# Five PSUM banks shared out anew between two kinds of attention scores in one layer

## The reference

```python
x = x + layernorm(attention(layernorm(x)))        # layer 1: 16 heads of 8, rotary, causal
x = x + layernorm(block2(layernorm(x)))
# block2: y = x + attention(rmsnorm(x))           # layer 2: 16 heads, latent keys (16) and 32 rotary columns
#         y + shared expert + top 2 of 8 experts, on rmsnorm(y)
```

## Time and profile before

| | |
|---|---|
| median of 3 runs | 577.48 us (576.83 to 578.33) |
| the profiled execution | 578.05 us, span 576.0 us |
| busy: PE, DVE, ACT, POOL | 507.3, 412.2, 313.7, 200.6 us |
| PE matmul instructions | 3168 |
| exps (L853) | 320, 600 ns each |
| maxima with mask (L1231) | 256, 638 ns each |
| plain reduces (L1221) | 96, 692 ns each |
| fills' matmuls, layer 1 (L530) | 256, 303 ns each |
| units' matmuls, layer 1 (L559) | 237 recorded, 295 ns each |
| HBM traffic | 80 GB/s over the span |

### The profile page before, as it was taken

How to read it: one execution, slowest core, us unless ns; L and a number is a source line. 1 busy time by engine, 2 the same in 40 slices (tenths; PEclk the granted TensorE clock), 3 DMA queues, 4 the chain that set the end, 5 groups by cost and what they waited for, 6 DMA issues and landing times.

```text
span 576.0 us, 9488 instructions
## 1 busy us (share of the span) xinstructions
PE 507.3 (88%) x3168; PEld 276.7 (48%) x3190; DVE 412.2 (72%) x1209; ACT 313.7 (54%) x586; POOL 200.6 (35%) x268
## 2 busy tenths in 40 slices
PE   7888988978899888999999999998989798899784
PEld 3433443433443344556565556554756346553643
DVE  6689898798589976876686688766476764554465
ACT  2485685767656775656756646543355342654131
POOL 5432643365236541564336414421032000410010
PEclk9999999999999999999999999999999899999978
DMA  5455524114223432448345542532203200000001
GB/s 139 128 147 172 149 82 138 43 44 135 77 80 117 155 72 90 91 115 171 103 99 108 121 127 91 129 46 52 53 15 66 55 2 1 20 2 0 2 1 37
DMA packets 29672, 47.17 MB, mean 82 GB/s; under 512 B 4648, under 2 KB 15144, under 8 KB 29112
## 3 DMA queue, kind: packets, MB, share of 16 engines
q1 hardware_dynamic: 28496, 45.72, 31.0%
q10 hardware_dynamic: 1128, 0.85, 0.7%
HBM read 27.22 MB, written 18.87 MB: 80 GB/s over the span
## 4 chain that ended last, share of the span: by engine, by line
PE 54%; DVE 27%; ACT 10%; issue 5%; POOL 3%; DVEq 0%; ACTq 0%; POOLq 0%
PE ps L612 11%; PE ps L565 9%; DVE ps L1231 8%; PE ps L686 8%; PE ps L532 6%; PE ps L530 4%; PE ps L820 3%; DVE NM L1221 3%; DVE terms L1337 2%; PE ps L550 2%; ACT PG L853 2%; PE ps L559 2%; PE ps L737 2%; PE ps L667 1%; DVE stats L1205 1%
## 5 line engine op out<-in xcount | busy, mean ns | idle before, releaser
L853 ACT ACTIVATE PG<-ps 128x512 f32<-128x512 f32 x320 | 179.4, 600 | 139.0 <-PE ps L565 87.7
L1231 DVE CUSTOM_DVE_ANT_0 ps<-ps,below 128x512 f32<-128x512 f32 (+1 forms) x256 | 157.1, 638 | 45.2 <-PE ps L532 22.6
L565 PE MATMUL ps<-QS,K 128*128 128x512 f32 x320 | 115.4, 445 | 3.0 <-ACT PG L853 2.9
L612 PE MATMUL ps<-PG,V 128*32 128x512 f32 (+3 forms) x1024 | 95.0, 444 | 3.1 <-DVE ON L1278 1.8
L532 PE MATMUL ps<-K,QS 96*128 96x256 f32 (+3 forms) x256 | 74.1, 341 | 10.2 <-DVE NM L1231 9.9
L1221 DVE TENSOR_REDUCE NM<-ps 128x2 f32<-128x512 f32 (+1 forms) x96 | 65.5, 692 | 22.1 <-PE ps L550 18.3
L530 PE MATMUL ps<-KS,QS 96*128 96x256 bf16 (+3 forms) x256 | 64.5, 303 | 17.3 <-DVE NM L1231 13.2
L565 PEld LDWEIGHTS ps<-QS,K 128*128 128x128 f32 x320 | 53.9, 189 | 44.1 <-ACT PG L853 23.1
L1066 POOL TENSOR_TENSOR rstd<-ve,half 128x4 f32<-128x4 f32 x20 | 20.4, 1018 | 117.4 <-DVE ve L1213 83.2
L1174 POOL TENSOR_SCALAR_AFFINE_SELECT PG<-PG 128x512 f32<-128x512 f32 x64 | 39.6, 641 | 57.4 <-ACT PG L853 57.0
L1167 POOL TENSOR_SCALAR_AFFINE_SELECT PG<-PG 128x512 f32<-128x512 f32 x64 | 38.7, 638 | 49.5 <-ACT PG L853 49.5
(11 more groups left out here) (170 smaller groups left out, 679.4 us busy)
## 6 DMA issues: line engine op xcount, KB each, us to landing
scr<-QC SPq DMA_DIRECT2D x24, 512.0 KB, 2.8
QS<-scr SPq DMA_DIRECT2D x64, 128.0 KB
scr<-room SPq DMA_DIRECT2D x20, 256.0 KB, 2.6
QS<-scr SPq DMA_DIRECT2D x15, 288.0 KB
KS<-scr SPq DMA_DIRECT2D x15, 288.0 KB
QS<-scr SPq DMA_DIRECT2D x64, 64.0 KB
x<-in_x SPq DMA_DIRECT2D x4, 256.0 KB, 3.3
out_x<-x SPq DMA_DIRECT2D x3, 256.0 KB, 2.3
```

The lines of the kernel that those rows point to most:

```text
L565: mm = pe.matmul(bank.rearrange("p (h q) -> p h q", h=HG), keys[:, SEQ[n] % 2, P * j:P * j + P], QS2[:, heads, P * i:P * i + P], start=(ke ...
L612: mm = pe.matmul(out, v, p, start=(j == 0), stop=(j == NT - 1), skip_group_check=True)
L853: act.activation(PG[:, n % 2, unit_place(LAYER[n], (u + k) % UNITS), :], ps[:, ST0 + (u + k) % 3, :], ACT.Exp, scale=scale).then_inc(exp_d ...
L1231: dve.tensor_tensor_reduce(out=bank[:, 0:w], in0=bank[:, 0:w], in1=below[:, T - w:T], scale=-1.0, scalar=-NEG, op0=ALU.add, op1=ALU.min, a ...
```

## The change

In layer 1 fills take the banks 0, 1 and 4 in turn and units the banks 2 and 3. From layer 2's first fill and unit on (fill 176 and unit 160), they take 0, 1 and 2, 3, 4 as before. The fills of group 16 are computed during group 14, so during groups 14 and 15 neither kind uses bank 4. The waits follow from the number of banks, and ScalarE and VectorE read the banks by the same functions.

```diff
+FILL_BANKS1 = (0, 1, 4)
+FILLS2, UNITS2 = FILLS * first_group(2, 0), UNITS * first_group(2, 0)
+
+def fill_depth(f):
+    return 3 if f < FILLS2 else 2
+
+def fill_bank(f):
+    return FILL_BANKS1[f % 3] if f < FILLS2 else (f - FILLS2) % 2
+
+def unit_depth(u):
+    return 2 if u < UNITS2 + 2 else 3
+
+def unit_bank(u):
+    return 2 + u % 2 if u < UNITS2 else 2 + (u - UNITS2) % 3
...
             def scores_for_max(n, hh, i):
...
-                if f >= 2:
-                    pe.wait_ge(fill_read, f - 1)
-                bank = ps[:, f % 2, :]
+                if f >= fill_depth(f):
+                    pe.wait_ge(fill_read, f + 1 - fill_depth(f))
+                bank = ps[:, fill_bank(f), :]
...
             def scores_for_exp(n, hh, i):
...
-                        for k in range(ST0, ST0 + 3):
+                        for k in (2, 3):
                             pe.wait_ge(bank_read[k], PRE_BANKS.count(k))
-                if u >= 3:
-                    pe.wait_ge(exp_done, u - 2)
-                bank = ps[:, ST0 + u % 3, :]
+                if u >= unit_depth(u):
+                    pe.wait_ge(exp_done, u + 1 - unit_depth(u))
+                if u == UNITS2 + 2:
+                    pe.wait_ge(fill_read, FILLS2)
+                bank = ps[:, unit_bank(u), :]
...
                     if m == 0:
                         pe.wait_ge(consts_ready, CONSTS)
-                        for k in range(2):
+                        for k in FILL_BANKS1:
                             pe.wait_ge(bank_read[k], PRE_BANKS.count(k))
```

More of the change, by code:

```diff
@@ L320, in block_program @@
         ps = ctx.enter_context(nc.psum_tensor("ps", [P, 8, T], F32))
-        ST0, BK_O = 2, 5
+        BK_O = 5
         loaded_first, loaded_qkv, loaded, x_loaded = sem("loaded_first"), sem("loaded_qkv"), sem("loaded"), sem("x_loaded")
@@ L852, in main @@
                         act.wait_ge(st_ready, u + k + 1)
-                        act.activation(PG[:, n % 2, unit_place(LAYER[n], (u + k) % UNITS), :], ps[:, ST0 + (u + k) % 3, :],
+                        act.activation(PG[:, n % 2, unit_place(LAYER[n], (u + k) % UNITS), :], ps[:, unit_bank(u + k), :],
                                        ACT.Exp, scale=scale).then_inc(exp_done, 1)
@@ L1226, in maximum @@
                 k = 2 * hh + hh // 2 + i
-                bank = ps[:, (n * FILLS + k) % 2, :]
+                bank = ps[:, fill_bank(n * FILLS + k), :]
                 if i < 2:
```

## The result

The changed kernel takes 588.77 us in the median of 4 runs, the kernel before 577.64 us beside it: a ratio of 1.020, with a 95% interval of 1.016 to 1.025. The forecast was slower, 581.3 us within 571 to 589, most likely 579.5 to 586. The direction was right; the loss of 11.1 us, in the second set 6.7, was foreseen as 3.8, so its size was not.

A forecast was written before the change was run, and what follows sets the result against it. TensorE was taken to bound the kernel, with VectorE nearly full in layer 1. The missing unit bank's 15.9 us less the third fill bank's 12.1 gave +3.8, so 581.3 us from 577.48, range 571 to 589.

The forecast's parts named there:

- What bounds layer 1, and the mechanism: Layer 1: TensorE first, VectorE nearly full; fill waits fall from 12.1 to under 3 us, exp waits rise to 12 to 20.
- the distances read group by group: Layer 1, each group's last unit waiting for exp 7: 24.2 us summed, less 5.3 that returns from old fill waits.
- VectorE's idle time at the plain reduces: Layer 1, a sign: new VectorE idle time before the next-to-last fill's plain reduces, 0.5 to 1.5 us in eight groups.
- I take the whole 12.1 us as gone: Layer 1: the third fill bank removes all 12.1 us of TensorE's array waits for maxima to free a bank.
- The section on whether the two are independent: Group 12 by its order: 11.3 us a group, 0.35 more than before; third fill bank pays most of the price.
- the 15.9 us: Layer 1, net price of the missing unit bank: 24.2 less 5.3 returned less 3.0 absorbed.
- the 3.0 us absorbed at the group borders: Borders into groups 9 and 14: TensorE waits there anyway, 1.8 and 1.2 us, so that much delay costs nothing.
- The small delays costed at nothing: Units 7 and 8, in some groups 2 to 4, late by some 0.5 us: counted as nothing, 4 us if uncovered.
- Groups 14 and 15: End of layer 1, bank 4 idle and two banks for each kind: cost nothing in group 14, 1.44 us in group 15.
- The fill banks win: Rival, layer 1: last unit's price only 6.5 us, fill banks gain the full 13.5, so 570.5 us; chance 0.24.
- They cancel: Rival, layer 1: price 15.9 against gain 13.5 and a little at the start, 577.5 to 579 us; chance 0.19.
- ScalarE becomes the bound of each group: Rival, layer 1: delay reaches nearly full VectorE, fills' gain halves to 6 us, small delays add 4; 591 us, chance 0.17.

The follow-up runs named there:

- e4: Changed kernel, but in layer 1 ScalarE takes exp 7 ahead of the output copy and the work beside it; 573.74 us, ratio 0.990 to the kernel before.
- e7: Changed kernel, but in layer 1 TensorE takes the group's last two fills ahead of its last unit; 574.78 us, ratio 0.992 to the kernel before.
- e12: The same kernel as e7, run again for an undisturbed trace; 577.60 us, ratio 0.994 to the kernel before.
- e1: Changed kernel, but with two fill banks and two unit banks in layer 1, bank 4 idle there; 594.76 us, ratio 1.031 to the kernel before.
- e5: Changed kernel unaltered, a second set of runs on another chip; 586.23 us against 579.50 for the kernel before, ratio 1.013.
- e13: e1 plus four matmuls into idle bank 4 ahead of the last unit in ten layer 1 groups; 589.03 us, ratio 1.017 to the kernel before.
- e14: e1 unaltered, on the same chip as e13; 595.42 us, ratio 1.029 to the kernel before.
- e8: Kernel before with its old banks, but exp 7 ahead of the output copy and the work beside it, as in e4; 582.48 us, ratio 1.006.
- e9: Kernel before with its old banks, but the group's last two fills ahead of its last unit in layer 1; 583.31 us, ratio 1.007.
- e2: Kernel before, but with three fill banks until the first unit, then the old banks; 577.86 us, ratio 0.999.

## Why the prediction was half right

**What bounds layer 1, and the mechanism: right.** TensorE's fill waits vanished, and exp waits took their place, at 22.0 us against 12 to 20 foreseen. E9's, once in 14 of the groups, are 18.3 of them; the distances read group by group gave 24.2 less 5.3, or 18.9. Layer 2 kept its length, and the difference lies in layer 1. Undoing the one order (e4) or the other (e7, e12) took the loss away. What was foreseen too small is VectorE's idle time at the plain reduces: 22.8 us in 24 waits of up to 2.4, not 0.5 to 1.5 in eight groups.

**The first step that failed: "I take the whole 12.1 us as gone".** The third fill bank was to bring 12.1 us; e1 against the changed kernel gives 6.3, because the wait at E9 lets VectorE catch up and leaves only 4.9 us of fill waits to remove. This alone is 5.8 of the 7.0 us that lie between the 3.8 foreseen and the 10.8 measured in layer 1. The section on whether the two are independent did follow them together for group 12, but the sum then went by the separate waits. That check had a step wrong too. It took everything up to OT as 1.4 to 1.5 us earlier, 11.3 us from one read of M9 to the next. In e5's trace, at the full clock, it is 12.1 (194.54 to 206.63), and OT comes 8.7 us behind the read of M9 instead of 9.4, so only 0.7 earlier. On the way the array has the new wait for VectorE's division, 0.7 us in this group of the first trace (3.3 in five over layer 1, 0.8 before).

**The second: the 15.9 us have no term for the clock.** The sum counted E9's wait as time in which nothing runs, and took the speed after it as given. The missing unit bank costs 17.1 us in e1, of which the clock is at least the 4.4 that e13 took away, so 12 to 13 by waiting. The waits of before for fills, 13.5 us in 30 pieces of up to 1.5, had not lowered the clock in layer 1; E9's come at 1.4 to 1.9 us in eight groups. Priced by e13 against e14, 4.4 us for four stretches of half clock, the changed kernel's five are 5 to 6 us (an estimate). Nor were the 3.0 us absorbed at the group borders: the wait of 1.2 us there is gone, the one of 1.8 us for xT is as long as before.

**The two errors hid each other.** Waiting alone is 10.8 less 5 to 6, about 5 us for the changed kernel by the first trace, against 3.8 foreseen. That this is close is luck: one term was 6 us too large, the other 3 to 4, and the clock's 5 to 6 us came on top. The time of 588.77 us lies just inside the range of 571 to 589, outside the likeliest 579.5 to 586.

**The small delays costed at nothing.** They are 3.7 us of array waits in layer 1, and were covered as supposed where that can be read: groups 3 and 4 of the changed kernel, whose E9 waits only 0.4 us, are 0.0 and 0.1 us longer than before. **Groups 14 and 15**: 0.0 and 1.1 us, against 0 and 1.44. **The start**: 0.4 us, within what was said.

**The rivals.** "The fill banks win" rested on the fills having nearly all of TensorE's idle time. By the rule that the prediction quotes from the Trainium skill (Perfetto Trace Analysis, Optimization Strategy), a repeated gap as a sign of too few buffers, the bank belonged there. The rule is right about the gap: with exp 7 first, the bank is worth 9.0 us. It doesn't see what the bank is taken from. "They cancel" is out by 10 us. "ScalarE becomes the bound of each group" named the larger loss, 591 us, and had two things right: the fills' gain is half (6 us), and the delay reached VectorE (22.8 us of waits). But its reason for the half, that VectorE is too full to win time back, is the opposite of what e1 shows, and VectorE was busy 156 of 209 us. Of the 4 us that it added for units 2 to 4, 0.9 us of waits are seen. The extra came from the clock.

**What stays open.** Why the new orders cost 3 to 4 us with the old banks (e8, e9) was not followed up. For e8 the copy to OT and all behind it comes later by an exp in each group, which would fit 201.1 against 198.1, but no run isolates it. Nor do the runs say why one E9 wait of 1.9 us is followed by a fall of the clock and the next is not: in the first trace of the changed kernel four of six are, in e1 three of six.

## What to carry to other kernels

A buffer that is hardly ever waited for may be what hides a burst on its reader: before taking it away, compare each writer's start with the end of the read one buffer back, look at what is queued behind the worst one, and whether the burst can be moved (here one exp placed earlier was worth 13.9 us of layer 1). A wait of TensorE that comes back in group after group can cost its length and then the clock, and two waits that face each other are not to be summed from the trace of before, as one feeds the other's slack.

## What the runs showed of the hardware

TensorE's clock often fell to its lower level right behind waits of 1.8 to 1.9 us, for 3.4 us each time, with 5 to 6 us to pay in layer 1 by the estimate above. Not each such wait was followed by a fall, and there were falls behind shorter ones: one in layer 1 of e4 has no wait over 0.7 us in the 6 us before it. In the trace of before the clock stayed at the upper level all through layer 1; the longest waits there are one of 1.8 us, at the border into group 9, and one of 1.5. In e2's, with the same banks in layer 1's groups, it fell behind that border wait, and group 9 is 0.9 us longer for it. Matmuls into an idle bank kept the clock up in the groups where they stood, and made the kernel faster by 6.4 us. And where the clock falls differs from run to run, so that one kernel on one chip spreads by 7 us (e4: 569.2 at a granted clock of 0.990, 576.4 at 0.977): a comparison of single runs should look at their clocks first.
